# Turning all of y by VectorE blocks and DRAM, and moving eight probability turns between TensorE and DRAM, in a fused attention and FFN block

## The reference

```
h   = layernorm(x)
q, k, v = h @ Wq, h @ Wk, h @ Wv                    # all 256 wide
att = softmax(causal(q @ k.T) / 16)                 # 1024 x 1024
y   = x + layernorm(att @ v @ Wo)
out = y + layernorm(layernorm(y) @ W[idx] + b[idx]) # idx: argmax of logits + gumbel(u)
```

## Time and profile before

| | us |
|---|---|
| median of 3 runs | 381.89 (381.63 to 382.5) |
| the profiled execution, its own time | 380.77 |
| span of the trace in it | 379.0 |
| TensorE busy | 365.0 (96%) |
| VectorE busy | 304.1 (80%) |
| ScalarE busy | 286.8 (76%) |
| GpSimd busy | 235.7 (62%) |

### The profile page before, as it was taken

How to read it: one execution, slowest core, us unless ns; L and a number is a source line. 1 busy time by engine, 2 the same in 40 slices (tenths; PEclk the granted TensorE clock), 3 DMA queues, 4 the chain that set the end, 5 groups by cost and what they waited for, 6 DMA issues and landing times.

```text
span 379.0 us, 7860 instructions
## 1 busy us (share of the span) xinstructions
PE 365.0 (96%) x2579; PEld 345.8 (91%) x2579; DVE 304.1 (80%) x728; ACT 286.8 (76%) x768; POOL 235.7 (62%) x412
## 2 busy tenths in 40 slices
...
DMA  6517988489956999479965989579984998114112
GB/s 220 155 32 236 235 236 221 127 262 274 245 182 196 246 266 274 140 254 257 259 222 173 237 253 272 163 243 232 261 281 111 268 255 216 57 67 116 57 55 85
DMA packets 54972, 75.23 MB, mean 199 GB/s; under 512 B 8724, under 2 KB 45844, under 8 KB 54036
## 3 DMA queue, kind: packets, MB, share of 16 engines
...
...
## 4 chain that ended last, share of the span: by engine, by line
PE 91%; DMA 3%; DVE 1%; ACT 1%; POOL 1%; issue 0%; POOLq 0%; ACTq 0%; SPq 0%; DVEq 0%
PE bank L1093 61%; PE score L1093 25%; DMA x_turn<-x_kept 2%; PE bank L1241 2%; DMA p_turn<-in_L_attn_Wk_dram 1%; PE score L1195 1%; PE bank L1148 1%; PE bank L1212 1%; POOL f_rstd L548 0%; DVE xT_lo L1022 0%; DVE xT_lo L868 0%; ACTq L816 0%; ACT f_junk L841 0%; SPq L445 0%; DVE f_sb L1060 0%
## 5 line engine op out<-in xcount | busy, mean ns | idle before, releaser
L594 POOL TENSOR_TENSOR pT_lo<-p_turn,pT_hi 128x640 fp32r<-128x640 f32 (+7 forms) x58 | 83.0, 1446 | 21.1 <-ACT pT_hi L769 20.3
L1093 PE MATMUL bank<-v_hi,pT_lo 128*128 128x258 f32 x288 | 81.8, 284 | 1.1 <-POOL pT_lo L594 1.1
L1093 PE MATMUL bank<-v_lo,pT_hi 128*128 128x258 f32 x288 | 81.3, 282 | 0.0
L1093 PE MATMUL bank<-v_hi,pT_hi 128*128 128x258 f32 x288 | 81.1, 282 | 0.0
L548 POOL TENSOR_TENSOR o_rstd<-o_ss,minus_half 128x1 f32<-128x1 f32 x64 | 39.1, 616 | 57.5 <-ACT o_junk L824 57.5
L1093 PE MATMUL score<-xT_hi,g_lo 128*128 128x384 f32 (+4 forms) x176 | 63.0, 358 | 0.0
L1093 PE MATMUL score<-xT_hi,g_hi 128*128 128x384 f32 (+4 forms) x176 | 61.2, 348 | 0.0
L1093 PE MATMUL score<-xT_lo,g_hi 128*128 128x384 f32 (+4 forms) x176 | 60.9, 346 | 0.0
L989 DVE CUSTOM_DVE_ANT_0 neg_scores<-score,mask 128x128 f32<-128x128 f32 (+3 forms) x64 | 47.6, 745 | 12.6 <-PE score L1195 7.8
L762 ACT ACTIVATE probs<-neg_scores,neg_max 128x128 f32<-128x128 f32 (+3 forms) x64 | 49.2, 772 | 11.0 <-DVE neg_max L989 6.6
L1093 PEld LDWEIGHTS bank<-v_hi,pT_lo 128*128 128x128 f32 x288 | 54.3, 189 | 2.3 <-DVE y L1039 1.3
...
## 6 DMA issues: line engine op xcount, KB each, us to landing
x_sb<-in_L_attn_x_dram SPq DMA_DIRECT2D x32, 256.0 KB, 3.5
out_dram<-f_sb SPq DMA_DIRECT2D x31, 256.0 KB, 4.4
...
x_turn<-x_kept ACTq DMA_DIRECT2D x28, 256.0 KB, 6.0
...
```

What stands on the lines that cost most here:

```text
L594: nc.gpsimd.tensor_tensor(p_half(pT_lo, b, n), p_quads(n), p_half(pT_hi, b, n).bitcast(f32), ALU.subtract).then_inc(p_lo_ready, 1)
L1093: last = nc.tensor.matmul(dst, l, r, start=(i == 0), stop=(i == len(passes) - 1))
```

## The change

All four y pairs of batches 0 to 6 are turned by VectorE blocks and DRAM; the last batch's own four stay on TensorE. In the last batch all eight probability tiles go through DRAM, and in batch 0 tiles 0 to 3 go over TensorE. All strings are written anew; the repeated ones and the start of the others:

```diff
-    PE_ORDER = """S0 S1 S2 S3 G2' G3' O6' O7' S4 Y2' S5 F0' S6 V0 V1 F1' Y3' S7 F2' F3' O0 O1 V2 V3 O2 O3 O4 G0 G1 O5"""
+    PE_ORDER = """S0 S1 O6' O7' S2 S3 S4 S5 F0' S6 S7 V0 F1' F2' V1 O0 O1 F3' V2 O2 V3 O3 O4 O5 G0 G1 G2 G3"""
-    POOL_ORDER = """C4' N0' C5' P6' P7' J0' L0 C6' C7' L1 J1' L2 L3 N1' N2' P0 U0' P1 P2 P3 N3' U1' C0 C1 P4 P5 C2 C3 U2'
-        U3'"""
+    POOL_ORDER = """N0' P6' P7' J0' C6' L0 C7' L1 N1' J1' J2' L2 L3 J3' U0' N2' P0 N3' P1 P2 U1' C0 C1 P3 P4 U2' C2 P5 C3 C4
+        C5 U3'"""
-    SP_ORDER = """Y1' A1' A2' P0 J1' P1 A3' Q0 Q1 P2 Q2 P3 Z0' Y0 Q3 J0 Z1' Z2' A0 Z3'"""
+    SP_ORDER = """J1' P0 J2' Y3' A3' Q0 P1 J3' P2 Q1 Q2 P3 Y0 Q3 A0 Z0' J0 Z1' Z2' A1 Y1 A2 Y2 Z3'"""
-    PE_LAST = """S0 S1 S2 T0 G2' S3 G3' O6' T1 T2 Y2' S4 O7' F0' S5 V0 T3 S6 F1' O0 S7 O1 V1 Y3' V2 F2' F3' O2 O3 Y0 V3
-        O4 T6 O5 F0 T7 O6 Y1 Y2 O7 F1 Y3 F2 Y4 F3 F4"""
+    PE_LAST = """S0 S1 O6' S2 S3 O7' S4 S5 F0' S6 S7 V0 V1 F1' V2 F2' O0 O1 O2 O3 F3' Y0 V3 Y1 O4 O5 F0 F1 O6 Y2 O7 F2 Y3
+        Y4 F3 F4"""
-    WARM = (22, 11, 17)
+    WARM = (22, 11, 22)
...
-                        dve.wait_ge(x_turned, b.count(NP, n + 1))
+                        dve.wait_ge(x_turned, min(b.count(NP, n + 1), NP * (B - 1)))
```

More of the change, by code:

```diff
@@ L61, in sandwich_block_kernel @@
     YS = 3
[L73 to L79, removed]
@@ L80, in sandwich_block_kernel @@
-    POOL_FIRST = """L0' L1' L2' L3' L0 L1 L2 L3 P0 P1 P2 C0 C1 C2 P3 C3 P4 P5"""
-    SP_FIRST = """I0 A0' A1' A2' A3' P0 Q0 P1 Q1 P2 Q2 P3 Y0 Q3 J0 A0"""
-    PE_ORDER = """S0 S1 S2 S3 G2' G3' O6' O7' S4 Y2' S5 F0' S6 V0 V1 F1' Y3' S7 F2' F3' O0 O1 V2 V3 O2 O3 O4 G0 G1 O5"""
[L83 to L86, removed]
@@ L87, in sandwich_block_kernel @@
-    POOL_ORDER = """C4' N0' C5' P6' P7' J0' L0 C6' C7' L1 J1' L2 L3 N1' N2' P0 U0' P1 P2 P3 N3' U1' C0 C1 P4 P5 C2 C3 U2'
-        U3'"""
-    SP_ORDER = """Y1' A1' A2' P0 J1' P1 A3' Q0 Q1 P2 Q2 P3 Z0' Y0 Q3 J0 Z1' Z2' A0 Z3'"""
-    PE_LAST = """S0 S1 S2 T0 G2' S3 G3' O6' T1 T2 Y2' S4 O7' F0' S5 V0 T3 S6 F1' O0 S7 O1 V1 Y3' V2 F2' F3' O2 O3 Y0 V3
-        O4 T6 O5 F0 T7 O6 Y1 Y2 O7 F1 Y3 F2 Y4 F3 F4"""
-    ACT_LAST = """G0' X2' G1' O4' X3' O5' E0 P6' P7' G2' T0 E1 E2 G3' O6' E3 J0' T1 N0' Y2' E4 T2 N1' N2' O7' F0' J1' N3'
-        E5 T3 V0 O0 F1' O1 V1 Y3' N0 V2 E6 P4 F2' P5 O2 F3' Y0 O3 E7 V3 O4 T6 O5 T7 F0 O6 Y1 N1 N2 N3 Y2
-        O7 Y3 F1 Y4 N4 F2 F3 F4"""
@@ L95, in sandwich_block_kernel @@
[L95 to L100, removed]
-    WARM = (22, 11, 17)
+    PE_FIRST = """I0 C0 I1 C1 A0 X0' X1' I2 G0' C2 X2' G1' X3' A1 S0 S1 G2' S2 G3' T0 S3 I4 S4 T1 S5 T2 T3 S6 S7 V0 V1 V2
+        O0 O1 V3 O2 O3 G0 O4 O5 G1 G2 G3"""
@@ new lines, in sandwich_block_kernel @@
+    ACT_FIRST = """C0 I0 H0' H1' A0 X0' X1' I1 H2' H3' G0' I2 X2' G1' X3' C1 I3 E0 G2' A1 I4 G3' E1 H0 H1 H2 H3 E2 E3 W0 T0
+        E4 E5 T1 T2 T3 D0 E6 V0 E7 V1 O0 V2 O1 I5 X0 X1 O2 P4 P5 V3 G0 X2 X3 N0 O3 O4 O5"""
+    DVE_FIRST = """L0' K0' I0 L1' K1' C1 L2' L3' K2' K3' A0 X0' X1' I1 I2 C2 G0' X2' G1' X3' L0 M0 L1 K0 L2 I3 M1 L3 K1 K2
+        G2' A1 G3' K3 M2 M3 I4 B0 B1 B2 B3 M4 M5 T0 Q4 Q5 C3 T1 T2 M6 M7 T3 Q6 V0 V1 Q7 V2 R0 I5 R1 X0
+        X1 N0 V3 R2 G0 X2 R3 R4 N1 X3 R5 N2 G1"""
+    POOL_FIRST = """L0' L1' L2' L3' L0 L1 L2 L3 C0 C1 C2 P4 P5 C3 C4 C5"""
@@ new lines, in sandwich_block_kernel @@
+    SP_FIRST = """A0' A1' A2' A3' I0 P2 Q2 P3 Y0 Q3 J0 A0 A1 Y1 A2 Y2"""
+    PE_ORDER = """S0 S1 O6' O7' S2 S3 S4 S5 F0' S6 S7 V0 F1' F2' V1 O0 O1 F3' V2 O2 V3 O3 O4 O5 G0 G1 G2 G3"""
+    ACT_ORDER = """P6' G1' G2' P7' J0' G3' E0 E1 N1' N2' O6' O7' H0 E2 J1' E3 E4 J2' E5 H1 N3' P0 P1 J3' H2 F0' H3 E6 V0 W0
+        E7 F1' P2 P3 P4 V1 O0 O1 D0 V2 F2' O2 P5 V3 F3' O3 X0 X1 O4 X2 O5 X3 N0 G0"""
+    DVE_ORDER = """M0 M1 Q0 Q1 L0 G2' L1 K0 G3' R6' K1 L2 M2 R7' N3' M3 B0 Q2 M4 Q3 M5 K2 Q4 Q5 L3 K3 F0' B1 M6 M7 B2 B3 Q6
+        F1' V0 Q7 F2' Z0' V1 Z1' R0 F3' R1 N0 V2 Z2' R2 V3 X0 X1 R3 R4 X2 X3 R5 Z3' G0 G1 N1 N2"""
```

7 lines of the change are left out of this document (added).

## The result

| | before | after |
|---|---|---|
| median (5 runs each, taken together), us | 381.88 | 384.64 |
| ratio, 95% interval | | 1.0092 [1.0061, 1.0123] |
| the profiled execution's span, us | 379.0 | 382.8 |
| first S0 to second S0, us | 38.4 | 38.1 |
| mean of the six periods, us | 43.35 | 44.94 |

The change makes the kernel slower by 0.9%. The forecast was 379.3 us, faster. The span grew by 3.9 us before rounding (378.98 to 382.84). With G2 and G3 of the first batch (2.86 us, now ahead of the second S0) put where they were before, the parts are: start -2.4, six periods +9.6, last batch -3.3.

What follows compares the result with a forecast made beforehand. TensorE, busy 365.0 of 379 us, was taken to bound the kernel; start -1.0, six periods +2.2 from late x and last batch -3.7 sum to -2.5 us, giving 379.3 us; range 371 to 388, the forecast's own 376 to 381.

Steps and rivals of the forecast that it cites:

- the trip: x's way through DRAM, from the write's issue to the first read of the fetched x; taken as 13.4 us.
- W: ScalarE's issue of the write of x to DRAM; taken at phase 22.2 of the period, range 22.2 to 22.8.
- the ends: First and last batch, outside the six periods; forecast to change by -1.0 us and -3.7 us.
- W plus trip = 36.0: Phase when x is back from DRAM; from there the six periods (+4.7 us) eat what the ends give.
- rival 2: Slower: y pair 3 or crowded DMA makes x later; period 45.1, +5.9 us in sum, 387.8 us; chance 0.25.
- hidden with about 1 us to spare: Claim that x's DRAM loop was hidden before with this slack and now sets the period.
- The loop S7, M7, B3, W, trip, lo, G0 to G3: TensorE product, VectorE row maximum and block turns, x through DRAM, its lo, TensorE's G quarters; period 43.7 us against 43.34.
- under 1 us ... paid only once with it: TensorE's possible bank waits at F3' or V2; lying ahead of G0, they are paid within its wait for x.
- a sign of another limit: TensorE waiting for something else, such as turned tiles or a bank, over 1 us each period would make the forecast wrong.
- rival 1: Nothing becomes late, the change saves what TensorE loses; period 42.46, -10.0 us in sum, 371.9 us; chance 0.25.
- The rule for one DMA: 2.0 us fixed plus bytes at 436 GB/s per DMA; gives a trip under 11 us, x never late.
- The last batch's cover: Remaining V and O work ahead of O6 and O7 hides tiles 6 and 7 through DRAM; if gone, up to 4 us.

Runs made afterwards that it cites:

- e2: Changed kernel with each of the four fetches of x bringing only a quarter of the bytes (not the whole computation): 376.84 us, 0.9859 to before.
- e4: Changed kernel with x going through DRAM in two halves, each with its own write and fetches: 379.81 us, 0.9972 to before.
- i1: Kernel before with all the last batch's probability tiles through DRAM and its last string reordered: 385.3 us, 1.0112 to before.
- i2: Like i1, on the kernel before, but the last batch's strings keep the old order: 392.32 us, 1.0294 to before.
- e3: Changed kernel with the write and fetches of probability tiles 6 and 7 moving a quarter of the bytes (not the whole computation): 379.93 us, 0.994 to before.
- j1: Changed kernel with the write of probability tiles 6 and 7 held until x's write has landed: 393.86 us, 1.0302 to before.
- e5: Changed kernel with y pair 3 of batches 0 to 6 turned on TensorE again: 388.12 us, 1.0189 to before.
- e1: Changed kernel with x pairs 2 and 3 turned before tile 7's row maximum and x's write issued earlier on ScalarE: 391.52 us, 1.0267 to before.
- f1: e4 with ScalarE's and VectorE's readings of some V and F banks moved earlier: 386.19 us, 1.017 to before.
- f2: Changed kernel, x's trip whole, with the same earlier bank readings as f1: 387.21 us, 1.0176 to before.
- g1: e4 with TensorE's V1 directly behind V0 and its bank read earlier on ScalarE and VectorE: 390.89 us, 1.0243 to before.
- j2: e4 with the write of probability tiles 6 and 7 held until the second half of x has landed in DRAM: 380.6 us, 1.0 to before.

## Why the prediction was wrong

**The step that failed** is the size of the trip in "The trip, from W's issue to the first read of x ... I take 13.4: x is there at 35.6". It measured 14.3. With W at 22.5 instead of 22.2, x came at phase 36.7. Of the 1.2 us by which the period missed (44.94 for 43.7), the trip is 0.9 and W 0.3; six times that is 7.4 us, and the ends, 1.0 better than forecast in sum, leave some 6.3 by which the span missed (382.8 for 376.5). The longer trip is a write 0.5 us longer and four issues of the fetch 0.8 longer, less 0.5 at its end. The issues are explained: the write of probability pair 3, 5.4 us behind the first fetch before, now starts 2.0 us ahead of it. The longer write isn't. The prediction had put the point from which the change loses at W plus trip = 36.0, and had the mechanism on both sides of it: this is rival 2 (chance 0.25), a little under its price (period 44.9 for 45.1). I took the trips of before as a property of the trip, though the same text says that the write and fetch of tiles 6 and 7 come some 6 us earlier in the phase and lie beside it. The bound was there and I kept the value of the other side. The text also calls the loop "hidden with about 1 us to spare", which its own sum contradicts (asked for at 38.3, there at 38.0); the rows of before give 0.1 to 1.0.

**What held.** The loop S7, M7, B3, W, trip, lo, G0 to G3 sets the period: with measured W and trip, the prediction's own sum 22.5 + 14.3 + 2.4 + 5.7 = 44.9 is the mean period. W's phase was 22.2 to 22.9 for the range of 22.2 to 22.8 that was given, from the two causes that were given. y pair 3 was back at phase 16.9 to 18.6, for 16.7 to 18.3. The last part gained 3.3 (forecast 3.7). The work taken out of a period is what was worked out: 42.57 without stops for 42.46. DMA is 84.5 MB, as worked out.

**What was off beside it.**
- The waits for banks "under 1 us ... paid only once with it". The second half holds while x is the later. But when x is in time (e2) they hold the period at 43.9 by themselves, and the stops cost more than their waits. In the changed kernel itself the waits for banks in the periods are 0.9 us a period, just under the 1 us that the prediction named as a sign of another limit. In these strings rival 1, with its 42.46, didn't come about with a short trip either (e2, e4), so its 0.25 was too much. With x in time the periods are still longer than before: 43.88 and 44.21 in e2 and e4 against 43.35.
- The start gained 2.4 where 1.0 was forecast. The wait of 2.1 for x is gone whole instead of halved (the first trip took 13.0 us for 15.2), and the 1.1 for a turned tile has made room for one of 1.3 for `v_lo`. The runs don't take the rest apart.
- The rule for one DMA that is set beside rival 1 stands in its section of the Trainium skill (DMA: Bandwidth & Descriptors, Anatomy of one DMA) for DMAs issued by GpSimd. Those of this trip are issued by ScalarE, so their length says little about that rule.
- The last batch's cover, priced at nothing, was there, but i1 and i2 show that it is the order that gives it.

**What stays open.** Why the write of x grew from 5.1 to 5.6 us: it isn't pair 3 of the probabilities (e3, j1) and not y pair 3 beside it, which is back before; e5 (5.21) shortens it but moves W and SyncE's fetches too. And no run shows whether the bank limit of 43.9 can be undone: four reorderings (e1, f1, f2, g1) moved waits and none removed them. No version that does the whole computation clearly beats the kernel before, the two best being e4 (0.9972 [0.9939, 1.0005]) and j2.
